# A fused attention and mixture-of-experts kernel: masks spread by transfers through memory, attention's steps ordered chunk by chunk, the first batch's stacks loaded by halves

## What is computed

```python
def attention_layer(x, ...):              # x [8, 1024, 256], 16 heads of 16 + 8 (rope) channels
    Qc = (x @ W_DQ @ W_UQ) ...            # per head 16, and rope(x @ W_DQ @ W_QR) per head 8
    Kc = (x @ W_DKV @ W_UK) ...           # per head 16, and rope(x @ W_KR), 8, shared by all heads
    scores = jnp.clip(einsum('bhqd,bhkd->bhqk', Q, K), -80.0, 80.0)
    scores = jnp.where(causal, scores, -inf)
    weights = softmax(scores / sqrt(24))
    return (weights @ V) @ W_O

def mixture_layer(x, ...):                # E, K, H, ITERS = 8, 2, 64, 2
    xf = x.reshape(8192, 256)
    logits = gelu(xf @ router_w1 + router_b1) @ router_w2 + router_b2
    topk_p, topk_i = top_k(softmax(logits), K)     # two experts of eight for each token
    for _ in range(ITERS):
        ctx = concatenate([integrated, v])         # 512 wide
        # each chosen expert e and a shared one: gelu(ctx @ w1[e] + b1[e]) @ w2[e] + b2[e], 768 wide,
        # of which x and v of the next step are made, weighed by topk_p and by a learned halt
    out = xf + integration_weight * (gelu(integrated @ refine_w1 + refine_b1) @ refine_w2 + refine_b2)

x = x + layernorm(attention_layer(layernorm(x)))
x = x + layernorm(mixture_layer(layernorm(x)))
```

## Time and profile before

| | us |
|---|---|
| median of 3 runs | 2783.69 |
| lowest and highest | 2780.39, 2785.09 |
| profiled execution, device time | 2781.41 |
| its span | 2779.7 |
| PE busy in the span | 2544.2 (92%) |
| DVE busy | 2272.2 (82%) |
| ACT busy | 1929.6 (69%) |
| POOL busy | 621.5 (22%) |

### The profile page before, as it was taken

How to read it: one execution, slowest core, us unless ns; L and a number is a source line. 1 busy time by engine, 2 the same in 40 slices (tenths; PEclk the granted TensorE clock), 3 DMA queues, 4 the chain that set the end, 5 groups by cost and what they waited for, 6 DMA issues and landing times. The chain is left out here.

```text
span 2779.7 us, 43055 instructions
## 1 busy us (share of the span) xinstructions
PE 2544.2 (92%) x16024; PEld 1787.8 (64%) x16024; DVE 2272.2 (82%) x3931; ACT 1929.6 (69%) x3075; POOL 621.5 (22%) x424
## 2 busy tenths in 40 slices
PE   3799899998999958999999999999999999999997
PEld 2233334333333336887888878888888887888997
DVE  4578887888877778798898889889988998887555
ACT  1687787877878836666676676666676767665886
POOL 2113121231212211111211121111111111110676
PEclk8899999999999978999999999999999999999999
DMA  3652644626445410000000000000000000001442
GB/s 99 87 97 72 103 96 84 106 69 105 93 86 95 114 46 1 1 16 16 1 16 16 8 8 16 16 1 16 16 16 1 16 16 9 1 8 51 136 137 76
DMA packets 125346, 136.75 MB, mean 49 GB/s; under 512 B 17122, under 2 KB 105186, under 8 KB 125140
## 3 DMA queue, kind: packets, MB, share of 16 engines
q1 hardware_dynamic: 125140, 134.00, 21.5%
HBM read 87.56 MB, written 46.40 MB: 48 GB/s over the span
## 5 line engine op out<-in xcount | busy, mean ns | idle before, releaser
L542 ACT ACTIVATE probs<-psum_a 128x1024 f32<-128x1024 f32 (+3 forms) x768 | 599.8, 816 | 210.7 <-PE psum_a L901 207.8
L1607 PE MATMUL psum_f<-w,picked 128*128 128x256 f32 (+1 forms) x2304 | 721.4, 346 | 0.0
L1606 PE MATMUL psum_f<-w,picked 128*128 128x256 f32 x2304 | 623.7, 288 | 1.2 <-DVE picked L1409 1.2
L1607 PEld LDWEIGHTS psum_f<-w,picked 128*128 128x128 f32 x2304 | 446.9, 194 | 53.4
L1606 PEld LDWEIGHTS psum_f<-w,picked 128*128 128x128 f32 x2304 | 447.3, 194 | 1.4 <-DVE picked L1409 1.4
L901 PE MATMUL psum_a<-q_stack,k_stack 72*128 72x512 f16 (+3 forms) x1536 | 378.4, 336 | 38.3 <-DMA q_stack<-q_rope_scratch 18.2
L618 DVE TENSOR_SCALAR probs<-probs 128x2048 f32<-128x2048 f32 (+3 forms) x320 | 320.1, 1000 | 84.9 <-ACT probs L542 84.8
L1234 ACT ACTIVATE gates<-psum_f 128x256 f32<-128x256 f32 (+1 forms) x384 | 186.1, 486 | 241.5 <-PE psum_f L1607 239.4
L916 PE MATMUL psum_a<-probs,v 128*17 128x512 f32 (+3 forms) x3072 | 334.2, 508 | 14.0 <-DVE probs L618 7.5
L1409 DVE TENSOR_TENSOR picked<-hid,masks 128x512 fp32r<-128x512 f32 x512 | 335.3, 715 | 13.1 <-PE psum_f L1607 10.0
L901 PEld LDWEIGHTS psum_a<-q_stack,k_stack 72*128 72x128 f16 x1536 | 98.2, 99 | 369.2 <-ACT probs L542 209.0
(11 more groups left out here) (298 smaller groups left out, 5373.8 us busy)
## 6 DMA issues: line engine op xcount, KB each, us to landing
heads_scratch<-kq_parts SPq DMA_DIRECT2D x64, 256.0 KB
k_stack<-heads_scratch SPq DMA_DIRECT2D x96, 128.0 KB
q_stack<-heads_scratch SPq DMA_DIRECT2D x96, 128.0 KB
x_in<-x_dram SPq DMA_DIRECT2D x8, 1024.0 KB, 5.5
x_res<-x_dram SPq DMA_DIRECT2D x16, 512.0 KB, 5.9
xs<-x_scratch SPq DMA_DIRECT2D x16, 512.0 KB, 3.9
xf_scratch<-xs SPq DMA_DIRECT2D x16, 512.0 KB, 2.9
xf<-xf_scratch SPq DMA_DIRECT2D x16, 512.0 KB, 6.1
```

What stands on the lines that cost most here:

```text
L542: act.activation(probs[:, s % PROB_SETS, 2 * u:2 * u + 2, q0:512], psum[:, 2 * u:2 * u + 2, q0:512], ACT.Exp, scale=exp_scale).then_inc(ex ...
L1606: pe.matmul(soft_out, x, cols[:, 1], start=start, stop=stop)
L1607: return pe.matmul(gate_out, x, cols[:, 2] if it == 0 else cols[:, 0::2], start=start, stop=stop)
```

## The change

Three things change.

- **Masks.** The jobs SP, the matrix `spread_w` with its two loads and two copies, and the copies of ACT and DVE to `masks` are gone. `mask_cols` becomes fp8 with two buffers. A new function `spread_masks(k)` on the SP queue waits for the copy of MT, writes the 8 x 512 rows of both slots to memory (2 transfers), waits until they are there, and reads them back into `masks` by 12 transfers, most of which broadcast a row over 64 or 128 partitions. Two places of `masks` that stay partly zero are cleared by POOL at the start. `pick` waits for the 12 transfers (`masks_in`) at the first unit of a block.
- **Order of attention's steps.** `steps` runs over chunks outside and groups inside: 16 diagonal steps of chunk 0, then 8 steps of chunk 1 for each group. The full steps stand at ticks 16 to 19, 24 to 27, 32 to 35 and 40 to 43. The jobs keep their ticks. `load_stacks(b, g)` now waits for step 23, 31, 39 or 47 of the batch before (it was 11, 23, 35, 47), and PE needs the stacks of groups 0 to 3 at ticks 0, 4, 8 and 12 (it was 0, 12, 24, 36).
- **First batch.** Its stacks are loaded by halves of 512 tokens, group 0 and then groups 1 to 3 at once. The first half is issued before x of the second batch, and before the second half has been computed.

The core of the diff:

```diff
-    steps = [(g, c, j) for g in range(GROUPS) for c in range(CHUNKS) for j in range(4 * c + 4)]
+    steps = [(g, c, j) for c in range(CHUNKS) for g in range(GROUPS) for j in range(4 * c + 4)]
-    last_step = [max(s for s in range(STEPS) if steps[s][:2] == divmod(ci, CHUNKS)) for ci in range(ACCS)]
+    last_step = [max(s for s in range(STEPS) if steps[s][:2] == (ci % GROUPS, ci // GROUPS)) for ci in range(ACCS)]
...
-                if b >= 2:
+                if b == 2:
+                    for i in range(2):
+                        sp.wait_ge(first_stacked[0][i], 16 * STACK_DMAS)
+                        sp.wait_ge(first_stacked[1][i], 16 * STACK_DMAS)
+                if b > 2:
-                        sp.wait_ge(stacked[g], 16 * STACK_DMAS * (b - 1))
+                        sp.wait_ge(stacked[g], 16 * STACK_DMAS * (b - 2))
...
-            def load_stacks(b, g):
-                if b > 0:
-                    sp.wait_ge(scores_ready, 2 * ((b - 1) * STEPS + last_step[CHUNKS * g + CHUNKS - 1] + 1))
-                hs = slice(4 * g, 4 * g + 4)
+            def stack(b, first, count, cols, done):
+                hs = slice(4 * first, 4 * (first + count))
-                        sp.dma_start(dst[row:row + dh, hs, :],
-                                     heads_dram[b % 2, f, part, 64 * g:64 * g + 64, :].rearrange("(h r) n -> r h n", r=dh)).then_inc(stacked[g], 16)
+                        sp.dma_start(dst[row:row + dh, hs, cols],
+                                     heads_dram[b % 2, f, part, 64 * first:64 * (first + count), cols].rearrange("(h r) n -> r h n", r=dh)).then_inc(done, 16)
-                    sp.dma_start(k_stack[row:row + dr, hs, :],
-                                 k_rope_dram[b % 2, part].unsqueeze(1).to_broadcast([dr, 4, SEQ])).then_inc(stacked[g], 16)
+                    src = k_rope_dram[b % 2, part, :, cols]
+                    sp.dma_start(k_stack[row:row + dr, hs, cols],
+                                 src.unsqueeze(1).to_broadcast([dr, 4 * count, cols.stop - cols.start])).then_inc(done, 16)
-                    sp.dma_start(q_stack[row:row + dr, hs, :],
-                                 q_rope_dram[b % 2, part, 32 * g:32 * g + 32, :].rearrange("(h r) n -> r h n", r=dr)).then_inc(stacked[g], 16)
+                    sp.dma_start(q_stack[row:row + dr, hs, cols],
+                                 q_rope_dram[b % 2, part, 32 * first:32 * (first + count), cols].rearrange("(h r) n -> r h n", r=dr)).then_inc(done, 16)
+            def load_first_stacks(half):
+                sp.wait_ge(scratch_written, 16 * SCRATCH_DMAS * (half + 1))
+                cols = slice(512 * half, 512 * half + 512)
+                stack(0, 0, 1, cols, first_stacked[half][0])
+                stack(0, 1, GROUPS - 1, cols, first_stacked[half][1])
+            def load_stacks(b, g):
+                sp.wait_ge(scores_ready, 2 * ((b - 1) * STEPS + last_step[GROUPS * (CHUNKS - 1) + g] + 1))
+                stack(b, g, 1, slice(0, SEQ), stacked[g])
...
+                if after == 0:
+                    load_first_stacks(0)
+                if after == 0:
+                    load_first_stacks(1)
+                if 0 < after < BATCH:
...
-                b, (g, c) = gci // ACCS, divmod(gci % ACCS, CHUNKS)
+                b, (c, g) = gci // ACCS, divmod(gci % ACCS, GROUPS)
...
-                    for r in (0, 64):
-                        dve.tensor_copy(late.spread_w[r:r + EXPERTS], late_raw[r:r + EXPERTS].rearrange("p (i n) -> p i n", i=5))
...
-                    pe.wait_ge(attn_ready, ACCS * b + CHUNKS * (GROUPS - 1) + half + 1)
+                    pe.wait_ge(attn_ready, ACCS * b + GROUPS * (half + 1))
...
-                if u == 0 and (c, j) == (0, 0):
-                    pe.wait_ge(stacked[g], 16 * STACK_DMAS * (b + 1))
+                if u == 0 and j == 0 and b == 0:
+                    pe.wait_ge(first_stacked[c][min(g, 1)], 16 * STACK_DMAS)
+                if u == 0 and (c, j) == (0, 0) and b > 0:
+                    pe.wait_ge(stacked[g], 16 * STACK_DMAS * b)
-                gci = b * ACCS + g * CHUNKS + c
+                gci = b * ACCS + c * GROUPS + g
...
-                [("HT", k, 0, 0), ("H", k, 0, 0), ("H", k, 0, 1), ("MT", k, 0, 0), ("SP", k, 0, 0)],
-                [("SP", k, 0, 1), ("SP", k, 0, 3), ("H", k, 0, 2)] + [("SP", k, 0, i) for i in (5, 2, 7, 4, 9, 6, 8)]]
+                [("HT", k, 0, 0), ("H", k, 0, 0), ("H", k, 0, 1), ("MT", k, 0, 0)],
+                [("H", k, 0, 2)]]
-        return job[0] in ("XT", "RT", "H", "LG", "HT") or job[0] == "SP" and job[3] % 2 == 0
+        return job[0] in ("XT", "RT", "H", "LG", "HT")
-        return job[0] in ("XT", "MT") or job[0] == "SP" and job[3] % 2 == 1
+        return job[0] in ("XT", "MT")
-        spread_w, lower_no = late.spread_w, late.lower_no
+        lower_no = late.lower_no
...
-        mask_cols = sb("mask_cols", [P, BLOCK], BF16)
+        mask_cols = sb("mask_cols", [P, 2, BLOCK], F8)
+        masks_cleared = sem("f_masks_cleared")
+        masks_written = sem("f_masks_written")
+        masks_in = [sem(f"f_masks_in{q}") for q in range(MASKS)]
+        MASK_DMAS = 12
+        mask_dram = nc.dram_tensor("mask_scratch", (2, 2, EXPERTS, BLOCK), F8, kind="Internal").ap()
...
+            def spread_masks(k):
+                dve_took(sp, ("MT", k, 0, 0))
+                if k >= 2:
+                    sp.wait_ge(masks_in[(k - 2) % MASKS], 16 * MASK_DMAS * ((k - 2) // MASKS + 1))
+                for s in range(2):
+                    sp.dma_start(mask_dram[k % 2, s], mask_cols[64 * s:64 * s + EXPERTS, k % 2]).then_inc(masks_written, 16)
+                sp.wait_ge(masks_written, 16 * 2 * (k + 1))
+                into, done = masks[:, k % MASKS], masks_in[k % MASKS]
+                for s, own, rows in ((0, 0, (64, 96)), (1, 7, (0, 32))):
+                    chosen_dram = mask_dram[k % 2, s]
+                    for h in range(2):
+                        sp.dma_start(into[64 * h:64 * h + 64, s, 1:4],
+                                     chosen_dram[1 + h:7 + h:2].unsqueeze(0).to_broadcast([64, FULL, BLOCK])).then_inc(done, 16)
+                    near, far = (0, 4) if s == 0 else (4, 0)
+                    sp.dma_start(into[:, s, far], chosen_dram[own].partition_broadcast(P)).then_inc(done, 16)
+                    sp.dma_start(into[64 * s:64 * s + 64, s, near], chosen_dram[own].partition_broadcast(64)).then_inc(done, 16)
+                    for r in rows:
+                        sp.dma_start(into[r:r + EXPERTS, s, near], chosen_dram).then_inc(done, 16)
+            sp.wait_ge(masks_cleared, 1)
+            for k in range(2):
+                spread_masks(k)
             for k in range(BLOCKS):
+                if k + 2 < BLOCKS:
+                    spread_masks(k + 2)
...
+            pool.memset(masks[:, :, 0, 0].bitcast(F32), 0.0)
+            pool.memset(masks[:, :, 1, 4].bitcast(F32), 0.0).then_inc(masks_cleared, 1)
-                if kind == "SP":
-                    s, place = divmod(i, 5)
-                    act.activation(masks[:, k % MASKS, s, place], src, ACT.Copy, saturate=False).then_inc(act_read, 1)
...
-                if k > 0:
-                    job_ready(dve, ("SP", k - 1, 0, 9))
-                dve.tensor_copy(mask_cols[:], bank(job)).then_inc(dve_read, 1)
-            def spread_rows(k, places):
-                for i in places:
-                    job = ("SP", k, 0, i)
-                    job_ready(dve, job)
-                    s, place = divmod(i, 5)
-                    dve.tensor_copy(masks[:, k % MASKS, s, place], bank(job), saturate=False).then_inc(dve_read, 1)
+                if k >= 2:
+                    dve.wait_ge(masks_written, 16 * 2 * (k - 1))
+                dve.tensor_copy(mask_cols[:, k % 2], bank(job), saturate=False).then_inc(dve_read, 1)
-                    act_took(dve, ("SP", k, 0, 8))
-                    dve_took(dve, ("SP", k, 0, 9))
+                    if it == 0:
+                        dve.wait_ge(masks_in[k % MASKS], 16 * MASK_DMAS * (k // MASKS + 1))
...
-            spread_rows(0, (1, 3, 5, 7, 9))
-                if t == 2 and kind == "first":
-                    spread_rows(k, (1, 3, 5, 7, 9))
```

## The result

The changed kernel takes 2743.45 us (median of 4, 2739.03 to 2754.03) against 2782.86 for the kernel before on the same chip: a ratio of 0.9865, 95% interval [0.9842, 0.9889]. It is faster, by 39 us, where I had forecast 99 us (2684); 2743 lies above my range of 2655 to 2725. The profiled execution took 2740.03, with a span of 2738.1 and a granted clock of 0.947.

The account below looks back on a forecast made before the run. PE was taken to bound mixture, DVE close behind; in attention either, by tick. Terms -75.5 - 31.5 - 2 - 1 + 8 + 0 + 3 - 1 = -100 took 2781.4 to 2681.4, median 2684; range 2655 to 2725.

Parts of the forecast that it names:

- Masks, on PE: Mixture: PE loses the mask products and the waits around them, 5.0 us a block, 15 times, 75.5 us.
- The coupling of DVE and PE, +8: Mixture: DVE and PE nearly level, lateness not always caught up; 0.5 us a block, 8 us in all, bounds 0 and +30.
- The clock, -31.5: Mixture: slow PE clock behind the mask products goes; 24 us over 15 blocks plus 7.5 in five, bound zero.
- the clock keeps falling once a block: Rival, mixture: the clock still falls each block since MT and HT remain; 28 us more, 2712; chance 12%.
- The transfers: Masks through memory: chain of 11.7 us in a window of 15.7, 27.4 if runs are dear; 2 us gained at mixture's start.
- Masks, on DVE: Mixture: DVE loses five copies, 3.4 us, and 3.7 us of waits a block, 94.0 to 86.9; `spread_w` copies save 1 more.
- Attention's order: Attention's steps paired otherwise: gains and losses by ticks sum to 0 a batch, bounds -14 and +14 over seven.
- the rival's direction: Rival, attention gets worse: short steps pile up behind DVE, first batch loses 10; 35 us more, 2719; chance 10%.
- mixture's terms, -102: Mixture's part of the sum: masks on PE -75.5, clock -31.5, mixture's start -2, `spread_w` copies -1, coupling +8.
- attention's, +2: Attention's part of the sum: order 0, stacks +3, first batch -1.
- The stacks' +3 (0 to 10): Attention: group 1's stacks land within a microsecond of their need at tick 4; 0.4 us a batch, +3 us.
- The first batch's account: Attention's start: `x_in` comes behind the stack loads at about 75, scores from 81 instead of 82.73; 1 us gained.

Follow-up runs that it names:

- lower_first: The changed kernel with DVE's lower parts of x for chunks 2 and 3 moved ahead of the pick, in 14 of 16 blocks; 2683.11 us, ratio 0.965.
- masks_only: The kernel before with only the masks' way through memory, attention left as it was; 2730.97 us, ratio 0.9819.
- attn_only: The kernel before with only attention's order by chunks and the first batch's halves, masks still by products; 2793.5 us, ratio 1.0043.

## Why the prediction was wrong

**Masks, on PE.** The place and the size were right. The products are gone, the slots stand right behind MT and H2, and where the pause is small the period is 87.3, against 87.4 forecast for PE alone and 87.9 with coupling. `lower_first` is in effect the kernel that I had costed, 2683.11 to my 2684. That the two agree to a microsecond is partly luck: attention cost more than I gave it, and the 87.3 hold 1.3 us of pause, so PE's own part was costed about a microsecond too dear.

**The coupling of DVE and PE, +8.** This is the step that failed. I compared sums over a period, DVE 86.9 and PE 87.4, and called what lies between them a matter of 0.5 us a block. In its place stood a pause of 3.7 us and, behind it, 2.4 us of slow clock. But PE and DVE meet in the middle of the period too, at the seam of the two groups, and there it is not the sums that count. The numbers to see it were on the table. I had found that the `integrate` at 2045.53 would start at 2041.5. Had I followed DVE from there, 25.5 us up to the lower parts at 2071.0, they would be done at 2067.0, or at 2066.1 if the wait of 0.9 us for ACT goes. PE would want them 5.0 + 1.6 us (its products and slow clock) before 2070.4, at 2063.8. That is a pause of 2.3 to 3.2 us, and it measured 3.7. The wait did go; the microsecond that DVE loses beside POOL was not in my account either, for in the trace before POOL's product ended at 2045.1, just ahead of this chain. I followed DVE's chain as far as the pick that needs the masks, since my question was when the masks were due, and stopped there.

**The clock, -31.5.** The mechanism was right, the count was wrong. I wrote that the slow clock follows waits which the change removes. It does, and the old ones are gone; a new and longer one came. Its slow stretch costs 2.4 us a block. My rival "the clock keeps falling once a block" had nearly the right effect (28 us) by the wrong reason: its MT and HT do not lower it, as `lower_first` shows. PE's own work at full clock is 85.8 us a block; 3.7 of pause, 2.4 of clock and 0.3 of small gaps make the 92.2. Against the 87.9 forecast that is 3.2 more for the coupling, 2.4 more for the clock and 1.3 less for all the rest of PE.

**The transfers.** Right. Chain 10.7 us against 11.7: the issues cost 0.54 us apiece and not 0.42, the stores landed 1.5 us behind their issue and not 2.9. No pick waits but the first. The Trainium skill's rule on partitions and ports ("SBUF — State Buffer", Door 1: the DMA port swizzle) agrees with this: runs of 512 bytes to 64 and 128 partitions were not dear, and the last landed 2.9 us behind its issue. Since the twelve issues alone took 6.5 us, no run here tells at what rate such runs can move. The start of mixture gained 1.9 + 1.6 us, where I had 3 and the block's share.

**Masks, on DVE.** DVE's busy time in a period fell from 85.2 to 82.0 us, 3.2 against the 3.4 forecast.

**Attention's order.** The sum of 0 in the middle batches holds for this execution (batches 1 to 6 take 695.4 us, 695.0 before), its parts only roughly. The windows of the fourth batch, to be held against the earlier trace rows: ticks 4 to 7, 12 to 15, 24 to 27, 28 to 31, 32 to 35.

```profile
430.92:441.56 10.64, 10.64 (x90) 6.06 (x91) 7.65 (x15) 7.54 (x13) 0.00 (x0) 1.00 0.67 103
...
453.29:467.12 13.83, 10.13 (x64) 3.87 (x65) 13.80 (x19) 6.88 (x11) 8.63 (x6) 0.75 0.25 77
...
486.14:497.99 11.85, 10.28 (x68) 3.67 (x70) 10.99 (x17) 9.55 (x12) 8.63 (x5) 1.00 0.37 125
497.99:506.60 8.61, 8.61 (x60) 2.74 (x61) 7.20 (x11) 5.90 (x9) 1.39 (x2) 1.00 0.00 1
506.60:517.01 10.41, 9.68 (x68) 3.60 (x70) 9.88 (x18) 10.00 (x14) 2.77 (x3) 1.00 0.39 129
```

They differ from before by -1.4 (forecast -1.9), -0.6 (+0.7), +1.9 (+1.0), -1.2 (-0.6), +0.7 (+1.2). Ticks 8 to 11 are 0.7 longer, not 0.5 shorter. The sign that I had wrong at 12 to 15 did no harm. What I did not see is the last batch, which has no projections to pair with: it takes 2.7 us longer. In the medians attention cost 12 us, in the rival's direction but a third of its size of 35, and within the bounds that I had given the order alone. By the medians the miss is thus in two parts: mixture's terms, -102 in my sum, came to -50 (`masks_only`), and attention's, +2, to +12 (`attn_only`).

**Stacks and first batch.** The stacks' +3 (0 to 10) held: waits of 0 to 5.4 us in the five traces with the halves and `x_in` behind them. The first batch's account held in every step, 2 to 3 us late: `x_in` behind the stacks, forecast for 75 and there at 77.9; scores from 81 on, and they stood at 82.98. The gain of 1 us became a loss of 0.3. The Trainium skill's rule on transfers with eight rows outside ("DMA: Bandwidth & Descriptors", Why a DMA increments its semaphore by 16 and not by 1) would have had `x_in` 6 us later than my 75, at 81; it came between the two, at 124 GB/s over the whole stretch, so this trace does not decide for it.

## What to carry to other kernels

When a stage loses work on its bounding engine, do not compare the engines' sums over a period; go to each place where that engine takes something from the next one, and follow the other engine's chain from its last real wait up to there. The new time of the first and the length of the second, less the waits in it that go too, give the pause, and the mend is often free: here two instructions moved ahead of a pick that nobody waited for brought more than the whole change. A pause that is long enough also costs clock, so the last microsecond of it can be worth three: here 1.2 us of pause, from 2.5 to 3.7, cost 3.6.

## What the runs showed of the hardware

The cost of a pause of PE is not linear. With the same work in all cases, pauses of 0.6 and 1.3 us left the granted clock at 1.00, one of 2.5 us did so in all blocks but one, and one of 3.7 us brought, each time, a stretch at 0.50. In the changed kernel's trace it began within the pause at all but the first of them and ended 5.3 to 5.8 us behind it; in the block shown it cost 2.4 us. How the length and the place of a pause act together stays open: in the kernel before the clock fell 1.5 us behind a stretch in which PE did seven products in 3.4 us and its longest gap was 1.3 us.

DVE's product of 768 columns took 1.95 us where POOL was at work when it began, and 0.96 without:

```profile
1924.39 0.95 DVE L1481 SCALAR_TENSOR_TENSOR terms<-gates,vs 128x768 f32<-128x768 f32 x1
1924.62 1.90 POOL L1218 TENSOR_TENSOR hid<-gel,hid 128x512 fp32r<-128x512 f32 x1 [9.21 <-ACT hid L1275]
1925.38 1.95 DVE L1482 TENSOR_TENSOR terms<-terms,soft_b 128x768 f32<-128x768 f32 x1
...
1939.88 0.96 DVE L1482 TENSOR_TENSOR terms<-terms,soft_b 128x768 f32<-128x768 f32 x1
```

In this trace all 14 products of this line that ran beside POOL took 1.94 to 1.95 us and the other 50 took 0.96; the product ahead, which had begun before POOL's, took 0.95. In the kernel before none of the 64 stood beside POOL, whose product there ended at 2045.1, ahead of the `integrate` at 2045.53. So in the changed kernel the two meet in the very chain that PE waits for. Its price, 1 of the 3.7 us of pause, is an estimate from these rows. Moving POOL's product out of the chain was not tried.
